# Rope in 128-partition pair tiles, and a head's projected result scaled by ScalarE copies with a per-partition scale

## The reference, cut to what matters

```python
x = x + deformable_conv(group_norm(x))              # x: 8 images of 64 channels, 32 x 32
t = tokens(x)                                       # 8 x 1024 tokens x 64
n = layer_norm(t)
q, k, v = n @ w_q.T, n @ w_k.T, n @ w_v.T           # 16 heads of 64
q, k = rope(q), rope(k)                             # pairs (a, b) -> (a*c - b*s, a*s + b*c)
att = softmax(where(causal, q @ k.T / 8, -inf))
t = t + (att @ v per head, heads side by side) @ w_o.T
t = t + spectral_ffn(layer_norm(t))                 # convolutions with 16 long filters
```

## Time and profile before

| | us |
|---|---|
| time, median of 3 runs (4390.66 to 4394.24) | 4394.03 |
| profiled execution: time | 4394.59 |
| profiled execution: span | 4392.8 |
| PE busy | 3431.4 |
| DVE busy | 2940.9 |
| ACT busy | 2272.4 |
| POOL busy | 2067.2 |

### The profile page before, as it was taken

The page is one execution under the profiler, slowest core; times in us unless marked ns, Lnnn a source line. Parts: engine busy times, 40 slices in busy tenths (PEclk is TensorE's granted clock), DMA queues, the critical chain, the costliest instruction groups (busy, mean ns, idle before and its releaser), DMA issues. The chain is left out here.

```text
span 4392.8 us, 64538 instructions
## 1 busy us (share of the span) xinstructions
PE 3431.4 (78%) x19824; PEld 2647.5 (60%) x19824; DVE 2940.9 (67%) x4313; ACT 2272.4 (52%) x3207; POOL 2067.2 (47%) x1576
## 2 busy tenths in 40 slices
PE   6233333333999999999999999999999958999998
PEld 1122222222666666676666667666666737898988
DVE  2344444444788888888888888888888865655646
ACT  0000000001677777777777777777777744554545
POOL 0577777775555555555555555555555540000000
PEclk8555555555999999999999999999999978999999
DMA  4533333333122222212122221222222132333333
GB/s 90 142 94 94 94 94 94 94 94 93 53 57 57 57 57 62 57 43 62 53 57 62 57 57 48 57 57 57 57 62 57 43 83 99 122 120 105 132 104 110
DMA packets 171257, 339.66 MB, mean 77 GB/s; under 512 B 61496, under 2 KB 78776, under 8 KB 170936
## 3 DMA queue, kind: packets, MB, share of 16 engines
q1 hardware_dynamic: 143544, 263.18, 20.6%
q0 software_dynamic: 27648, 75.53, 5.9%
HBM read 246.09 MB, written 24.38 MB: 62 GB/s over the span
## 5 line engine op out<-in xcount | busy, mean ns | idle before, releaser
L1033 DVE TENSOR_TENSOR attention_probs_l<-attention_probs,attention_probs_h 128x896 fp32r<-128x896 f32 (+4 forms) x768 | 843.0, 1098 | 65.0 <-ACT attention_probs_h L942 64.8
L938 ACT ACTIVATE attention_probs<-attention_pss 128x896 f32<-128x896 f32 (+4 forms) x768 | 623.7, 812 | 476.0 <-PE attention_pss L804 469.2
L991 DVE TENSOR_REDUCE attention_mx<-attention_pss 128x1 f32<-128x256 f32 (+7 forms) x1032 | 728.5, 746 | 197.2 <-PE attention_pss L820 196.3
L415 POOL DMA_INDIRECT deform_gat<-table,deform_idx x576 | 671.3, 1166 | 208.0 <-issue 170.6
L942 ACT ACTIVATE attention_probs_h<-attention_pss 128x896 fp32r<-128x896 f32 (+4 forms) x768 | 620.4, 808 | 0.0
L1043 POOL TENSOR_TENSOR attention_qk<-attention_tA,attention_tB 128x512 f32<-128x512 f32 x260 | 417.7, 1607 | 368.6 <-DVE attention_tB L1001 336.8
L817 PE MATMUL attention_pss<-attention_KA,attention_QA 128*128 128x512 f32 (+2 forms) x1548 | 480.9, 400 | 102.1 <-DMA attention_QA<-attention_QA 86.4
L1484 DVE SCALAR_TENSOR_TENSOR spectral_eo<-spectral_psE,spectral_sig,spectral_eo 64x512 fp32r<-64x512 f32 x512 | 383.9, 750 | 263.8 <-ACT spectral_eo L1463 259.2
L1075 POOL TENSOR_TENSOR kept_T<-kept_T,attention_scaled 128x512 f32 x129 | 206.2, 1598 | 713.3 <-DVE attention_scaled L980 673.6
L801 PE MATMUL attention_pss<-attention_QA,attention_KA 128*128 128x512 f32 (+4 forms) x1536 | 496.6, 377 | 20.6 <-ACT attention_probs_h L942 12.7
L1387 PE MATMUL spectral_psE<-spectral_tz,spectral_up 128*128 128x256 f32 (+2 forms) x3072 | 507.5, 324 | 4.4 <-DVE spectral_eo L1484 4.4
(11 more groups left out here) (174 smaller groups left out, 5656.8 us busy)
## 6 DMA issues: line engine op xcount, KB each, us to landing
spectral_tz<-phis SPq DMA_DIRECT2D x128, 320.5 KB, 4.6
spectral_tz<-phis SPq DMA_DIRECT2D x128, 320.0 KB, 4.2
attention_xb<-xn SPq DMA_DIRECT2D x67, 512.0 KB, 4.7
attention_wt<-wsplit SPq DMA_DIRECT2D x67, 512.0 KB, 5.4
attention_KB<-attention_KA SPq DMA_DIRECT2D x130, 256.0 KB, 3.4
attention_QA<-attention_QA SPq DMA_DIRECT2D x130, 256.0 KB, 3.5
table<-offsets_pixT SPq DMA_DIRECT2D x32, 288.0 KB
deform_gat<-table,deform_idx POOLq DMA_INDIRECT x576
```

What stands on the lines that cost most here:

```text
L415: pool.indirect_dma_start(gat[:, r, k, :, :].rearrange("p q c -> p (q c)"), None, d.table.rearrange("r q c -> r (q c)"), bass.IndirectOffs ...
L938: act.activation(probs[:, j % 2, 0:width], pss[:, slot, lead:lead + width], ACT.Exp, scale=float(E) ** -0.5)
L991: ins = dve.tensor_reduce(mx[:, nh % 2, i:i + 1], pss[:, slot, first:first + (i + 1) * P], AX.X, ALU.max)
L1033: dve.tensor_tensor(probs_l[:, cols], probs[:, j % 2, 0:widths(j)], probs_h[:, cols].bitcast(F32), ALU.subtract).then_inc(s_lo, 1)
```

## The change

The rope's rounded copy is made once for both heads: ScalarE copies 128 x 512 to a new tile `nat_h`, GpSimd subtracts 128 x 512 into `nat_l`, and every part of `KA`, `KB`, `QA` and `QB` is filled from the two by DMA, half a row (512) at a time: 24 transfers of a 64 x 512 block for a pair of heads, where there were 4 of 64 x 1024. The `out` unit is read by ScalarE: VectorE only takes the reciprocal, ScalarE makes eight copies of 128 x 64 with the reciprocal as per-partition scale. The steps, units, `PV_AT` and `UPPER_AT` have a new order. The units are the same ones, with the same matmuls.

```diff
-STEPS = [(0,), (2,), (3,), (1,), (4, 5), (7, 6)]
+STEPS = [(0,), (7, 6), (1,), (3,), (2,), (4, 5)]
...
-    0: [[("rope", 0)], [("rope", 1), ("max", 5)], [("max", 7), ("rope", 2)], [("rope", 3), ("max", 4, 1), ("max", 0, 6)],
-        [("max", 3, 2)], [("out",), ("row",)]],
-    1: [[("max", 1, 5)], [("max", 7), ("max", 4, 2)], [("max", 3, 0)], [("max", 6)], [("out",), ("row",)], []],
+    0: [[("max", 0, 6), ("rope", 0), ("max", 5, 1), ("rope", 1)], [("rope", 2)], [("max", 3, 2)], [("rope", 3), ("max", 4)],
+        [("max", 7)], [("out",), ("row",)]],
+    1: [[("max", 4, 2)], [("max", 3, 1), ("max", 7)], [], [("max", 5, 0)], [("max", 6)], [("out",), ("row",)]],
...
-PV_AT = {(0, "end"): -2, (1, "end"): -1, (3, "before"): 0, (4, "before"): 1, (5, "after"): 2, (5, "end"): 3}
+PV_AT = {(0, "before"): -2, (1, "after"): -1, (2, "end"): 0, (4, "before"): 1, (4, "after"): 2, (5, "end"): 3}
...
-UPPER_AT = {1: 0, 2: 1, 3: 2, 4: 3}
+UPPER_AT = {0: 0, 2: 1, 3: 2, 4: 3}
...
-BY_ACT = ("S", "row")
+BY_ACT = ("S", "row", "out")
...
+                    if u[0] == "out":
+                        scale_out(slot, h % 2, BODY_HEADS * it + h)
...
+                def scale_out(slot, buffer, before):
+
+                    out = pss[:, slot, :].rearrange("p (t c) -> p t c", t=NT)
+                    wait_apart(act, s_T, before + 1, s_apart)
+                    act.wait_ge(s_rec, before + 1)
+                    for t in range(NT):
+                        ins = act.activation(scaled[:, buffer, t, :], out[:, t, 0:E], ACT.Copy, scale=rec[:, buffer, t:t + 1])
+                    ins.then_inc(s_act, 1)
...
                     act.wait_ge(s_sum, R + r + 3)
-                    act.activation(dst[0:E, 2 * pp, cols], qk[0:E, r % 2, :], ACT.Copy)
-                    act.activation(dst[E:P, 2 * pp + 1, cols], qk[E:P, r % 2, :], ACT.Copy).then_inc(s_H, 1)
+                    act.activation(nat_h[:, r, :], qk[:, r % 2, :], ACT.Copy).then_inc(s_H, 1)
...
-                    dve.reciprocal(rec[:, :], out[:, :, E]).then_inc(s_rec, 1)
                     wait_apart(dve, s_T, before + 1, s_apart)
-                    dve.wait_ge(s_rec, before + 1)
-                    dve.tensor_tensor(scaled[:, buffer, :, :], out[:, :, 0:E],
-                                      rec[:, :].unsqueeze(2).to_broadcast([P, NT, E]), ALU.mult).then_inc(s_dve, 1)
+                    dve.wait_ge(s_full, n + 1)
+                    dve.reciprocal(rec[:, buffer, :], out[:, :, E]).then_inc(s_rec, 1)
...
+                    pool.tensor_tensor(nat_l[:, r, :], qk[:, r % 2, :], nat_h[:, r, :].bitcast(F32),
+                                       ALU.subtract).then_inc(s_low, 1)
```

More of the change, by code:

```diff
@@ L548, with half_steps @@
 FIRST_MAX = [[u for units in UNITS[h] for u in units if u[0] == "max"][0] for h in range(2)]
+def half_steps(half):
+    steps = [j for j, tiles in enumerate(STEPS) if any(t // 4 == half for t in tiles)]
+    return steps[0], steps[-1]
+HALF_STEPS = [half_steps(half) for half in range(2)]
 BODY_HEADS = 4
-UPPER_AT = {1: 0, 2: 1, 3: 2, 4: 3}
+UPPER_AT = {0: 0, 2: 1, 3: 2, 4: 3}
 SLOTS = 3
 PV_LAG = 2
-PV_AT = {(0, "end"): -2, (1, "end"): -1, (3, "before"): 0, (4, "before"): 1, (5, "after"): 2, (5, "end"): 3}
+KQ_COPIES = 16 * (2 * 6 + 2 * 4)
+PV_AT = {(0, "before"): -2, (1, "after"): -1, (2, "end"): 0, (4, "before"): 1, (4, "after"): 2, (5, "end"): 3}
 LEAVE_AT = 1
@@ L757, in _ @@
                 load(1, 0, 1)
-                for w in range(2):
-                    copy(0, w, 2 * w + 4)
+                for r in range(4):
+                    copy(0, r, 0)
                 sp.wait_ge(s_full, 4)
@@ L766, in _ @@
                         for pp, last_rope in ((1, rope1), (0, rope0)):
-                            for w in range(2):
-                                copy(pp, w, 8 * it + (4 * (2 - pp) + 2 * w + 4))
+                            for r in range(4):
+                                copy(pp, r, 8 * it + 4 * (2 - pp))
                             sp.wait_ge(s_full, it * N_BODY + (N_AHEAD + last_rope + 1))
@@ L860, in pv @@
                         pe.wait_ge(s_y, BODY_HEADS * it + h + 1)
-                    if h == 0 and STEPS[j][0] in (0, 4):
-                        pe.wait_ge(s_xt[STEPS[j][0] // 4], 16 * b + 16)
+                    for half in range(2):
+                        if h == 0 and j == HALF_STEPS[half][0]:
+                            pe.wait_ge(s_xt[half], 16 * b + 16)
                     for kt_ in STEPS[j]:
@@ L1003, in unit @@
                     if u[0] == "out":
-                        scale_out(slot, h % 2, before)
+                        invert_sums(slot, n, h % 2, before)
                 def split_maxima(h, seen, before):
@@ L1043, in add, with lower, pair @@
                     pool.tensor_tensor(qk[:, r % 2, :], tA[:, r % 2, :], tB[:, r % 2, :], ALU.add).then_inc(s_sum, 1)
-                def lower(r, R, pp):
-                    w, c = divmod(r, 2)
-                    cols = slice(c * HB, (c + 1) * HB)
+                def lower(r, R):
                     pool.wait_ge(s_H, R + r + 3)
                     pool.wait_ge(s_sum, R + min(r + 2, 4) + 2)
[L1052 to L1058, removed]
-                    pool.sem_inc(s_L, 1)
-                def pair(reads, R, pp):
+                    pool.tensor_tensor(nat_l[:, r, :], qk[:, r % 2, :], nat_h[:, r, :].bitcast(F32),
+                                       ALU.subtract).then_inc(s_low, 1)
+                    pool.wait_ge(s_low, R + r + 1)
+                def pair(reads, R):
                     add(0, reads[0], R)
@@ L1076, in add_out @@
                                        ALU.add).then_inc(s_T, 1)
-                pair(range(1, 5), 0, 0)
+                pair(range(1, 5), 0)
                 ropes, outs = places("rope"), places("out")
```

62 lines of the change are left out of this document (37 added, 25 removed).

## The result

The changed kernel takes 4593.1 us (median of 4 runs, 4587.89 to 4595.73) against 4394.1: a ratio of 1.045, 95% interval 1.0435 to 1.0471, so 4.5% slower. The direction was forecast, with 4506 us; the time lies above the range of 4350 to 4575.

A forecast was written before the change was run, and what follows sets the result against it. TensorE, busy 92% of the attention, was taken as the bound, so only its idle time could move. Sum: 4394.6 - 206 (old waits) + 224 (copies) + 68 (S0's slot) + 26 (late reciprocal), forecast 4506 us, range 4350 to 4575.

The forecast's parts named there:

- the queue: End of each head: eight scaled copies precede ScalarE's copy of the maxima, so TensorE waits 1.75 us, 224 us in all.
- the slot waits of before: Two waits a pair for an exponential that frees a PSUM slot, taken as 1.1 us a pair; they go.
- the unit that needs S0's slot: Start of an even head: waits 0.42 us, and once in two pairs 1.28 more for a table load; 68 us.
- All that can move is TensorE's idle time: TensorE's matmuls stay the same in another order; removing its idle time could win at most 206 us.
- The copies: Eight scaled copies on ScalarE behind the reciprocal, taken not to overlap: 8 x 0.304 = 2.43 us.
- The reciprocal: VectorE's reciprocal in an even head, up to 0.8 us late beside GpSimd's last `lower`; 26 us, bounds 0 and 51.
- 224 + 26 us of the sum: 224 us for TensorE's wait ahead of every head's first `S`, 26 us for the late reciprocal in even heads.
- The transfers: DMA copies of Q for an odd head's first `max`: no wait taken, upper end 58 us.
- I am wrong: Holds if the eight copies take under 1.6 us, or if `S` is not released by the copy of the maxima.
- The transfers are late: Rival: 24 issues fill SyncE's queue, transfers land at the upper end, reciprocal 0.8 us late; 4589 us, chance 0.10.
- The copies are short: Rival: eight copies take 1.6 us or less; 4400 us at 1.6, 4352 at 1.0; chance 0.22, half of it faster.
- The waits vanish: Rival: TensorE has a missed reserve ahead of the first `S`, so 206 - 68 us are won; 4256 us, chance 0.05.

The follow-up runs named there:

- run 7: The new rope alone in the kernel before (old order, scaling by VectorE): 4400.9 us, ratio 1.0016.
- run 3: Fourteen idle matmuls added on TensorE ahead of the first `S` of odd heads in the changed kernel: 4519.8 us, ratio 1.0292.
- run 1: The changed kernel with VectorE scaling the projected result again, order and rope as changed: 4541.1 us, ratio 1.0336.
- run 10: The changed kernel with Q's upper copies issued first and GpSimd's last two subtractions held behind the even head's reciprocal: 4445.4 us, ratio 1.0117.
- run 5: The scaling by ScalarE alone in the kernel before (old order, old rope): 4521.6 us, ratio 1.0289.
- run 11: The kernel before with the new rope, Q's upper copies issued first and the scaling by ScalarE: 4550.8 us, ratio 1.0359.
- run 12: The changed kernel with a constant scale of 0.5 in the eight copies, normalisation left out: 4523.1 us, ratio 1.0292.

## Why the prediction was wrong

**The bound, and the queue, were right.** TensorE sets the time; the copy of the maxima behind the eight copies holds every first `S`; the slot waits of before are gone, and the unit that needs S0's slot comes 0.50 us late (due 2068.24, there 2068.74), and 1.75 us with the table load: forecast 68 us, by the rows 32 x 0.50 + 32 x 1.75 = 72.

**The step that failed** is "All that can move is TensorE's idle time", and with it "I lay out one pair in the new order with durations from the rows". Those durations are TensorE's at 2.4 GHz, and every idle time got its own length as its price; the clock has no term in the sum. TensorE's busy time moved too, by 47 us. Wherever the clock fell behind a wait, the head took some 1.5 us more (run 7: 17.6 against 16.1 us): 73 us in all by run 3, of the 87 that the forecast is short. The attention of before, with no idle time over 1.2 us on TensorE, doesn't show it.

**Two terms were mis-sized and nearly cancel.** *The copies*: 2.43 us taken, 1.58 and 1.77 measured. The row that the sum leaned on the earlier trace rows doesn't carry over: its copies alternate between the halves of the partitions, and eight on the same 128 partitions overlap. That the halves are the reason was argued as a rival and fits, but width and output type differ as well, and no run tells them apart. The estimate of 1.9 us by the figures of the Trainium skill ("ScalarE: Activation LUTs", What ACT_TABLE_LOAD costs) was the nearer: these copies are 328 ns long and 0.20 us apart, where its formula gives an estimate of 332 ns and 0.24 us.

*The reciprocal*: at most 0.8 us late in an even head was allowed for and 0.4 priced; 1.6 was measured. In an odd head `S` comes 5.07 us behind the projection's start (2060.30 to 2065.37) and in an even one 6.47; forecast were 5.77 and up to 6.57. So the 224 + 26 us of the sum are 208 + 33 by the rows. The 208 are the waits of the first `S`: 1.92 us behind an even head, 1.15 behind an odd one, and 1.5 where an iteration begins. The 33 are a wait of 0.5 us of one `pv` in an even head for VectorE's late `probs_l`, which was not foreseen.

**The transfers** make TensorE wait 0.45 us a pair in the timeline, 29 us, inside the bounds of 0 to 58; the sum took 0. Their placing was off by more than that. SyncE's queue at the end of the pair:

```profile
2040.11 2.45 SPq L762 DMA_DIRECT2D attention_QA<-attention_nat_h  x4
2042.61 1.23 SPq L770 DMA_DIRECT2D attention_QB<-attention_nat_l  x2
2043.95 2.46 SPq L762 DMA_DIRECT2D attention_QA<-attention_nat_h  x4
2046.45 1.24 SPq L770 DMA_DIRECT2D attention_QB<-attention_nat_l  x2
```

The prediction counts six issues, to end 3.7 us behind the projection's start. Ten had to go out, since the four of unit 2's copies were issued at this time too, and the last that matters ends at 2046.41, 6.2 us behind it. The wait stayed short only because `S` was late itself; run 1 shows the 2.31 us that it is otherwise.

Sum with measured terms: 4394.6 - 206 + 208 + 33 + 72 + 29 + 73 = 4604, 11 us over the median and 16 over the profiled execution, from whose rows the terms are.

**The signs that were named.** `S` is released by the copy of the maxima in every head, and the third unit of an even head waits, as written; the DMA wait of the earlier trace rows, which was to go, shrank. But the eight copies take 1.58 us in even heads, just under the 1.6 that was to mean "I am wrong", and ScalarE's busy share of the attention is 67%, where up to 77% was forecast.

**The rivals.** "The transfers are late" named 4589 us, which is near the result by chance: the wait for transfers is half of what it took, and the clock fills the gap. "The copies are short" was right on the copies (1.6 us) and wrong on the outcome (4400), since it kept the reciprocal early and knew no fall of the clock. "The waits vanish" is refuted.

**What the parts do.** Scaling alone +130, order alone +205, rope alone +9, all three +199 us: they don't add up. The new order needs the quick rope and lost with it as well. The rope gains 83 us in the old order as soon as Q's upper copies are issued first. The scaling by ScalarE loses wherever it was tried: 130 us, 52 us and 242 us. The new order with VectorE's scaling, Q's upper copies first and GpSimd held back, all three, was not run, so what this order is worth at its best stays open.

## What to carry to other kernels

On the engine that sets the time, price an idle time by its length and by what the clock does behind it; a filler matmul (run 3), or a wait on another engine (run 10), can win time there. Before work is moved to an engine that is 70% busy, look at what stands behind it in that engine's queue: here a copy that the bound engine waits for. And a queue of transfers is an order too: issue first what is waited for first.

## What the runs showed of the hardware that was not expected

- The granted clock fell from 1.00 to one half for some 3.5 us behind idle times of TensorE, and the length of the idle time alone doesn't decide. From 1400 to 3400 us it fell behind 39 of 47 waits of 1.8 us (changed kernel), 27 of 49 of 2.0 us (run 5), 33 of 49 of 2.1 us (run 11), 6 of 52 of 1.4 us (run 7) and none of 52 of 1.1 to 1.2 us (kernel before). In run 10 it fell once behind waits of 0.95 and 0.54 us close together.
- Copies of 128x64 from PSUM with a per-partition scale are 328 ns long and 0.20 us apart in a row; with a constant scale 250 ns and 0.11 apart (run 12). Copies of 64x512 that alternate between the halves of the partitions don't overlap, 0.69 us apart.
- An eight-column cast on VectorE took 1.14 us beside a GpSimd subtraction, 0.17 without; a 768-column subtraction 2.02 and 0.96. The Trainium skill ("SBUF — State Buffer", SBUF: two separate sides) says that the two engines share a pair of ports, which one of them holds for a whole instruction, VectorE only for some kinds of instruction. The trace agrees: the slow cast ends at 2041.70, and the first of GpSimd's two subtractions (2040.40, 2.64 us for both) by an estimate of half their time at 2041.72.
- SyncE took 0.61 us to issue a 64x512 transfer, 12 in 7.6 us at a pair's end (2040.11 to 2047.69), where it took 0.55 for one of 64x1024: half the size saved nothing there.
